# New instruction orders on four engines and a masked bias table in one GpSimd operation, in an attention and mixture-of-experts kernel

## What is computed

```python
xn = _layernorm(x)
# attention: scores times a 0/1 lower-triangular mask (masked scores are 0, not minus infinity)
q, k, v = xn @ Wq.T, xn @ Wk.T, xn @ Wv.T
attn = softmax((q @ k.T) * tril / sqrt(512)) @ v
# experts: the best 2 of 8 gates, renormalised
y[e] = xn @ We[e] + be[e]
ffn = sum over the two kept experts of gate[e] * y[e]
out = x + attn + ffn
```

## Time and profile before

| | before |
|---|---|
| median of 3 runs | 123.94 us (123.93 to 124.2) |
| the profiled execution's own time | 124.14 us |
| its span | 122.3 us |
| granted TensorE clock, mean | 0.998 |
| PE busy | 114.8 us, 94% of the span |
| weight loads (beside PE) | 103.6 us, 85% |
| VectorE (DVE) busy | 106.0 us, 87% |
| ScalarE (ACT) busy | 100.2 us, 82% |
| GpSimd (POOL) busy | 91.4 us, 75% |

### The profile page before, as it was taken

One profiled execution on the slowest core, in us unless ns is written; L12 is line 12 of the kernel. 1 busy time (PEld: TensorE's weight loads), 2 busy tenths in 40 slices (PEclk: granted clock), 3 DMA queues, 4 the chain that ended last, 5 costly groups with the idle time before them and its releaser, 6 DMA issues.

```text
span 122.3 us, 2940 instructions
## 1 busy us (share of the span) xinstructions
PE 114.8 (94%) x735; PEld 103.6 (85%) x735; DVE 106.0 (87%) x533; ACT 100.2 (82%) x338; POOL 91.4 (75%) x185
## 2 busy tenths in 40 slices
PE   4988959999999999999999999999999999989991
PEld 4857657998899998998899998999899989978890
DVE  0699858999989999898989998999989897869992
ACT  2465498989997999799987998799987999949950
POOL 7419848589947998499848996699849994677990
PEclk9999999999999999999999999999999999999999
DMA  3769400000200012000300020000300020000023
GB/s 98 245 195 300 106 3 5 0 3 3 86 0 0 3 29 62 0 0 3 91 3 0 0 82 9 0 0 5 88 0 0 5 86 0 0 3 0 21 73 86
DMA packets 9233, 5.18 MB, mean 42 GB/s; under 512 B 384, under 2 KB 9088, under 8 KB 9216
## 3 DMA queue, kind: packets, MB, share of 16 engines
q1 hardware_dynamic: 8656, 4.66, 13.4%
q10 hardware_dynamic: 560, 0.33, 1.0%
HBM read 2.89 MB, written 2.10 MB: 41 GB/s over the span
## 4 chain that ended last, share of the span: by engine, by line
PE 70%; POOL 11%; DVE 7%; ACT 5%; issue 3%; DMA 2%; POOLq 1%; DVEq 0%; ACTq 0%
PE attb L305 12%; PE ring L247 11%; PE ring L251 11%; PE ring L248 11%; PE score L292 5%; PE score L251 3%; PE score L248 3%; PE score L247 3%; PE ring L323 2%; DMA x_all<-in_x_dram 2%; POOL ysc L1097 2%; PE ring L333 2%; ACT ysc L905 2%; POOL rhs_rows L1136 2%; PE attb L357 1%
## 5 line engine op out<-in xcount | busy, mean ns | idle before, releaser
L905 ACT ACTIVATE ysc<-ring,gate 128x128 f32<-128x128 f32 x124 | 35.6, 385 | 1.8 <-PE ring L251 1.6
L247 PE MATMUL ring<-w_hi,xT_hi 128*128 128x512 f32 (+2 forms) x96 | 34.8, 363 | 0.0
L251 PE MATMUL ring<-w_hi,xT_lo 128*128 128x512 f32 (+2 forms) x96 | 32.7, 340 | 0.2 <-DVE xT_lo L508 0.2
L248 PE MATMUL ring<-w_lo,xT_hi 128*128 128x512 f32 (+2 forms) x96 | 32.5, 339 | 0.0
L1094 POOL TENSOR_TENSOR ysc<-ysc 128x256 f32<-128x256 f32 x31 | 22.8, 735 | 13.0 <-ACT ysc L905 13.0
L1097 POOL TENSOR_TENSOR ysc<-ysc,mix 128x256 f32<-128x256 f32 x31 | 22.8, 735 | 4.4 <-DVE mix L575 2.1
L575 DVE SCALAR_TENSOR_TENSOR mix<-ring,gate,mix 128x128 f32<-128x128 f32 x65 | 22.3, 345 | 0.4
L305 PE MATMUL attb<-c_s,probT 128*128 128x128 f32 x152 | 22.5, 278 | 0.0
L305 PEld LDWEIGHTS attb<-c_s,probT 128*128 128x128 f32 x152 | 20.4, 192 | 0.9
L247 PEld LDWEIGHTS ring<-w_hi,xT_hi 128*128 128x128 f32 x96 | 18.1, 189 | 2.4 <-DVE mix L575 0.5
L924 ACT ACTIVATE prob<-score,nmx 128x128 f32<-128x128 f32 (+3 forms) x32 | 17.7, 554 | 2.6 <-DVE nmx L624 1.8
(11 more groups left out here) (114 smaller groups left out, 242.3 us busy)
## 6 DMA issues: line engine op xcount, KB each, us to landing
x_all<-in_x_dram SPq DMA_DIRECT2D x7, 256.0 KB, 4.3
out_dram<-o_s SPq DMA_DIRECT2D x7, 256.0 KB, 2.3
w_f<-in_w_stacked_dram SPq DMA_DIRECT2D x1, 256.0 KB, 4.4
w_f<-in_w_stacked_dram SPq DMA_DIRECT2D x1, 192.0 KB, 4.2
w_f<-in_w_stacked_dram SPq DMA_DIRECT2D x1, 132.0 KB, 3.2
x_all<-in_x_dram ACTq DMA_DIRECT2D x1, 128.0 KB, 2.9
x_all<-in_x_dram SPq DMA_DIRECT2D x1, 128.0 KB, 2.7
wqk_s<-in_w_attention_dram ACTq DMA_DIRECT2D x1, 128.0 KB, 3.4
```

Of the source, the lines that this page charges most:

```text
L247: nc.tensor.matmul(dst, hi, w_h, start=True, stop=False)
L248: nc.tensor.matmul(dst, hi, w_l, start=False, stop=False)
L251: return nc.tensor.matmul(dst, lo, w_h, start=False, stop=True)
L905: last = nc.scalar.mul(ysc[:, t, e, :], bank(f"A{t}", b)[:, e * P:(e + 1) * P], gate[:, b % 2, t, e:e + 1])
```

## The change

The `WARM` counts go from 6 and 4 to 8 and 1. The bank order and the orders of PE, DVE, ACT and POOL are new in all three phases. At the start, B's low part moves from VectorE to GpSimd and A's high part moves ahead of batch 0's tokens on ScalarE. Batch 1's load waits for C's landing instead of B's, and the loads of batches 2 to 7 now wait for A's. `bias_rhs` becomes `bias_rhs_split` (a copy, a product and a sum over all 128 partitions) and `bias_rhs_blocks` (one product with four mask columns, behind the power for batch 1); the four 32-partition sums and the clearing of `rhs_rows` go. In the loop each engine's instructions per stage stay the same. The core of the diff, with the inner functions that only wrap the same code left out:

```diff
-WARM = (6, 4)
+WARM = (8, 1)
...
-FIRST_GROUPS = """C0@0 U@0 C1@0 C2@0 C3@0 SV@0 B0@0 A0@0 X@1 A1@0 B1@0 C0@1 C1@1 U@1 C2@1 A2@0""".split()
-GROUPS = "B2- C3 A3- B3- SV DT- A0 B0 X+ A1 B1 C0+ U+ C1+ C2+ A2".split()
-LAST_GROUPS = """B2@-2 C3@-1 A3@-2 B3@-2 DT@-2 SV@-1 A0@-1 B0@-1 A1@-1 B1@-1 B2@-1 A2@-1 B3@-1 A3@-1 DT@-1""".split()
+FIRST_GROUPS = """C0@0 C1@0 U@0 C2@0 C3@0 SV@0 B0@0 A0@0 X@1 A1@0 B1@0 U@1 C0@1 A2@0 C1@1 C2@1""".split()
+GROUPS = "B2- C3 A3- B3- SV DT- B0 A0 X+ A1 B1 U+ C0+ C1+ A2 C2+".split()
+LAST_GROUPS = """B2@-2 C3@-1 A3@-2 B3@-2 A0@-1 B0@-1 DT@-2 B1@-1 B2@-1 A1@-1 A2@-1 B3@-1 SV@-1 DT@-1 A3@-1""".split()
...
-        be_s = sb("be_s", [P, P + 1])
+        be_s = sb("be_s", [P, P + 1 + NT])
...
-            sp.wait_ge(S["w_b"], 16)
+            sp.wait_ge(S["w_c"], 16)
             sp.dma_start(x_all[:, NT * P:2 * NT * P].rearrange("p (t d) -> p t d", d=P), x_v[1]).then_inc(S["x1"], 16)
+            sp.wait_ge(S["w_a"], 16)
...
 
             wide(0, "C", 0)
+            wide(0, "C", 1)
             project_u(0)
-            wide(0, "C", 1)
             wide(0, "C", 2)
             wide(0, "C", 3)
+            value_sums(0)
             scores(0, 0)
             scores(0, 1)
-            value_sums(0)
             wide(0, "B", 0)
+            scores(0, 2)
             wide(0, "A", 0)
+            transpose_x(1)
             transpose_probs(0, 0)
-            scores(0, 2)
+            wide(0, "A", 1)
+            transpose_probs(0, 1)
             scores(0, 3)
-            transpose_x(1)
+            wide(0, "B", 1)
+            project_u(1)
+            wide(1, "C", 0)
+            wide(0, "A", 2)
             attend(0, 0)
-            wide(0, "A", 1)
-            wide(0, "B", 1)
-            wide(1, "C", 0)
-            transpose_probs(0, 1)
             wide(1, "C", 1)
-            project_u(1)
             wide(1, "C", 2)
 
             for n in range(1, B - 1):
                 wide(n - 1, "B", 2)
                 wide(n, "C", 3)
+                attend(n - 1, 1)
+                scores(n, 0)
+                transpose_probs(n - 1, 2)
                 wide(n - 1, "A", 3)
-                attend(n - 1, 1)
+                transpose_probs(n - 1, 3)
                 wide(n - 1, "B", 3)
-                transpose_probs(n - 1, 2)
-                scores(n, 0)
-                transpose_probs(n - 1, 3)
                 attend(n - 1, 2)
+                value_sums(n)
                 scores(n, 1)
-                value_sums(n)
                 transpose_rows(n - 1)
                 attend(n - 1, 3)
                 bias(n - 1)
+                wide(n, "B", 0)
                 wide(n, "A", 0)
-                wide(n, "B", 0)
                 scores(n, 2)
+                transpose_probs(n, 0)
                 transpose_x(n + 1)
-                transpose_probs(n, 0)
                 wide(n, "A", 1)
                 wide(n, "B", 1)
+                scores(n, 3)
+                project_u(n + 1)
...
-                wide(n + 1, "C", 0)
                 transpose_probs(n, 1)
-                project_u(n + 1)
                 wide(n + 1, "C", 1)
-                scores(n, 3)
                 wide(n + 1, "C", 2)
-                wide(n, "A", 2)
 
             wide(B - 2, "B", 2)
             wide(B - 1, "C", 3)
             scores(B - 1, 0)
             transpose_probs(B - 2, 2)
             wide(B - 2, "A", 3)
...
             scores(B - 1, 3)
             wide(B - 1, "B", 1)
+            attend(B - 2, 2)
             wide(B - 1, "B", 2)
-            transpose_probs(B - 1, 1)
+            attend(B - 2, 3)
+            wide(B - 1, "A", 1)
+            bias(B - 2)
             wide(B - 1, "A", 2)
             wide(B - 1, "B", 3)
+            transpose_probs(B - 1, 1)
+            value_sums(B - 1)
+            transpose_probs(B - 1, 2)
+            transpose_probs(B - 1, 3)
+            attend(B - 1, 0)
+            transpose_rows(B - 1)
             wide(B - 1, "A", 3)
-            transpose_probs(B - 1, 2)
-            attend(B - 1, 0)
-            transpose_probs(B - 1, 3)
             attend(B - 1, 1)
-            transpose_rows(B - 1)
             attend(B - 1, 2)
             bias_early(B - 1)
...
+            def first_sums(b):
+
+                dve.wait_ge(S["low_ready"], 1)
+                dve.wait_ge(S["xh_ready"], 1)
+                nc.vector.tensor_reduce(xs[:, 1:NT - 1], late_x[:, early].rearrange("p (t k) -> p t k", k=P), AX_X, ALU.add)
+                nc.vector.tensor_reduce(xs[:, 0:1], bank("X", 0)[:, P:2 * P], AX_X, ALU.add).then_inc(S["xsum_ready"], 1)
+
...
-            early, late = slice(0, 2 * P), slice(2 * P, NT * P)
-            dve.wait_ge(S["xh_early_ready"], 1)
-            split_lo(xT_lo[:, 0, early], bank("X", 0)[:, early], xT_hi[:, 0, early], S["xl_early_ready"])
-            dve.wait_ge(S["xh_ready"], 1)
...
+            first_sums(0)
+            x_lo_half(0, 1)
             normal_stats(1, 0)
             token_sums_pairs(0)
             normal_stats(1, 1)
             normal_stats(1, 2)
             normal_stats(1, 3)
+            normal_finish(1)
+            token_sums_later(0)
             u_lo(0)
-            token_sums_later(0)
-            normal_finish(1)
+            gate_max(0)
+            gate_drop(0)
             mask_scores(0, 0)
-            gate_max(0)
+            mask_scores(0, 1)
+            gate_below(0)
             negate_max(0, 0)
-            gate_drop(0)
-            gate_below(0)
+            negate_max(0, 1)
+            sv_rows(0, 0)
+            sv_rows(0, 1)
             gate_sum(0)
-            sv_rows(0, 0)
+            sv_rows(0, 2)
             gate_rec(0)
             gate_out(0)
-            sv_rows(0, 1)
-            sv_rows(0, 2)
             mix_b(0, 0, 0)
             mix_b(0, 0, 1)
-            mask_scores(0, 1)
             mix_b(0, 0, 2)
-            negate_max(0, 1)
             x_lo(1)
             token_sums(1)
...
                 mix_b(n - 1, 1, 0)
                 mask_scores(n - 1, 2)
                 mix_b(n - 1, 1, 1)
+                negate_max(n - 1, 2)
                 mix_b(n - 1, 1, 2)
-                negate_max(n - 1, 2)
-                token_sums_pairs(n)
+                u_lo(n)
                 normal_stats(n + 1, 0)
-                u_lo(n)
                 normal_stats(n + 1, 1)
+                normal_stats(n + 1, 2)
                 mask_scores(n - 1, 3)
-                token_sums_later(n)
                 mix_b(n - 1, 2, 0)
-                normal_stats(n + 1, 2)
                 mix_b(n - 1, 2, 1)
-                normal_stats(n + 1, 3)
                 negate_max(n - 1, 3)
                 mix_b(n - 1, 2, 2)
                 gate_max(n)
+                normal_stats(n + 1, 3)
                 gate_drop(n)
                 softmax_sum(n - 1)
+                token_sums_pairs(n)
                 softmax_tot(n - 1)
+                token_sums_later(n)
                 gate_below(n)
+                normal_finish(n + 1)
+                mix_b(n - 1, 3, 0)
                 mask_scores(n, 0)
-                softmax_rec(n - 1)
-                mix_b(n - 1, 3, 0)
-                normal_finish(n + 1)
+                mix_b(n - 1, 3, 1)
                 gate_sum(n)
                 negate_max(n, 0)
-                mix_b(n - 1, 3, 1)
+                mix_b(n - 1, 3, 2)
                 gate_rec(n)
+                softmax_rec(n - 1)
                 gate_out(n)
                 mask_scores(n, 1)
-                mix_b(n - 1, 3, 2)
-                negate_max(n, 1)
-                finish_tile(n - 1, 0)
                 sv_rows(n, 0)
                 sv_rows(n, 1)
+                mix_b(n, 0, 0)
                 sv_rows(n, 2)
+                mix_b(n, 0, 1)
+                finish_tile(n - 1, 0)
+                mix_b(n, 0, 2)
                 finish_tile(n - 1, 1)
-                mix_b(n, 0, 0)
+                negate_max(n, 1)
                 finish_tile(n - 1, 2)
-                mix_b(n, 0, 1)
                 finish_tile(n - 1, 3)
-                mix_b(n, 0, 2)
                 x_lo(n + 1)
                 token_sums(n + 1)
...
             softmax_sum(B - 1)
+            softmax_rec(B - 2)
             softmax_tot(B - 1)
+            mix_b(B - 1, 1, 2)
+            mix_b(B - 1, 2, 2)
+            finish_tile(B - 2, 0)
+            finish_tile(B - 2, 1)
+            finish_tile(B - 2, 2)
             mix_b(B - 1, 3, 0)
-            mix_b(B - 1, 2, 2)
+            finish_tile(B - 2, 3)
             mix_b(B - 1, 3, 1)
             mix_b(B - 1, 3, 2)
+            sv_rows(B - 1, 0)
+            sv_rows(B - 1, 1)
             softmax_rec(B - 1)
             mix_a(0)
+            sv_rows(B - 1, 2)
             mix_a(1)
             mix_a(2)
-            mix_a(3)
             finish_tile(B - 1, 0)
             finish_tile(B - 1, 1)
+            mix_a(3)
             finish_tile(B - 1, 2)
             finish_last(B - 1)
...
...
+            a_high(0)
+            wa_high(0)
+            x_hi_half(0, 0)
```

(80 more changed lines are left out.)

125 lines of the change are left out of this document (62 added, 63 removed).

## The result

The changed kernel takes 120.13 us (median of 4 runs, 120.04 to 120.22) against 123.94 us before (median of 4, 123.59 to 124.2): a ratio of 0.969, 95% interval 0.967 to 0.972, so 3.8 us or 3.1% faster. The forecast had the sign and the mechanism of the start right and was too small: 121.8 us, with 120.8 as the lower end of its range.

A forecast was written before the change was run, and what follows sets the result against it. The prediction took TensorE to bound the loop, with visible waits only in the start and end. Its terms, -1.4 (start), -0.3 (loop) and -0.4 (end), summed to -2.1 us: 121.8 us against 123.94, range 120.8 to 123.7.

The forecast's parts named there:

- Term 1: Start: earlier low part of A, power and batch 1 transposes, -1.4 us, ends 0.3 and 1.8 us of gain.
- (a): Start: GpSimd's subtraction for A's low part begins at 7.5 us instead of 8.88, 1.4 us earlier.
- (b): Start, GpSimd before the power: 2.4 us of bias table and B's low part replace 3.33 us, 0.9 less.
- (c): Start: power for batch 1 at 11.2 us instead of 13.51, so transposes possible at 14.4 instead of 16.70.
- (d): Start: TensorE is ready for batch 1's transposes at about 14.4 us; its earlier 0.61 us wait grows to about 1.2.
- Term 2: Six loop stages: the new order gains 0.05 us a stage, -0.3 us; lower end -1.0.
- Term 3: End: the 0.51 us wait for batch 6's bias rows goes, last A product later, -0.4 us; ends -0.9 and +0.5.
- slower rival: Loop: the third value row comes too late for the transposes in every stage, 125.7 us; chance 0.13.
- little start: Start: VectorE decides when batch 0's banks come free, nothing gained in loop and end, 123.4 us; chance 0.12.
- unchanged case: Start: normalisation stays where it was, loop at TensorE's pace as before, 123.9 us; chance 0.07.
- all of it at once: Whole kernel: 1.8 us from the start, 1.0 from the loop, 0.5 from the end, 120.7 us; chance 0.08.
- first products at half rate: Start: C triples and U at 1.2 GHz take 2.1 us more, about half hidden: 0 to +1.0, taken as 0.

The follow-up runs named there:

- e7: The kernel after with the old bias table in place of the new, ahead of B's low part and the power: 122.09 us.
- e2: The kernel before with the new loop orders of TensorE, VectorE and ScalarE and the loop's new bank order: 123.11 us against 124.04.
- e8: The kernel after with VectorE's pair sums and token sums moved back to about their old places in each stage: 120.30 us.
- e3: The kernel before with the change's end on all four engines: 123.25 us against 124.04.
- e11: The kernel before with the new loop orders of VectorE and ScalarE, TensorE's old: 132.96 us, ratio 1.070.
- e1: The kernel before with the change's start on all engines, including loads, dummy matmuls and bias table: 122.72 us against 124.04.
- e5: The kernel before with the value sums moved ahead of attend(n-1, 2) in TensorE's loop: 124.29 us against 123.95.
- e6: The kernel before with scores(n, 3) moved ahead of project_u(n+1) in TensorE's loop: 125.37 us, ratio 1.011.
- e4: The kernel before with TensorE's new loop order and its banks alone: 131.71 us, ratio 1.062.
- e9: The kernel after with ScalarE's loop order of the kernel before: 126.70 us, ratio to before 1.021.
- e10: The kernel after with VectorE's loop order of the kernel before: 122.86 us, ratio to before 0.989.
- e12: The kernel after with the sum of the bias split moved behind the power for batch 1: 120.42 us, ratio to before 0.970.

## Why the prediction was right or wrong

**What bounds the kernel**: right as far as it went. The loop goes at TensorE's pace in both kernels, and the start and the end had the visible waits. Wrong was the reading that the loop had no waits of TensorE, and that the room of the other engines was worth nothing there.

**Term 1, the start, -1.4**: right, measured -1.69 on the traces. (a) 7.60 us for a forecast of 7.5. (b) 1.3 us for the three operations up to 10.13 and 1.00 for B's part, for a forecast of 1.4 and 1.0. (c) the power at 11.20, as forecast; the variance was ready only then, held up behind B's part on GpSimd (0.75 us for an operation of 0.17, the row at 10.36), a wait that the prediction did not have. (d) the transposes at 14.33 for 14.4, with TensorE there at the same time; its wait ahead of the value sums was 0.94 us, for 1.2. The first B product came at 20.13 for 20.2 to 20.6: the 0.1 taken off for VectorE behind the transposes was not needed. Run e7 shows the term's main part directly, 1.96 us.

**Term 2, the loop, -0.3**: this is the step that failed; it measured -1.49. The prediction counted 13.1 us from the columns against 13.47, had the room of 0.35 us a stage (its own numbers give 0.37, 2.2 us over six), and then gave it away with the sentence "since the windows show no idle TensorE, I expect most of the 0.35 to be short matmuls that don't reach 0.454 ns a column, not waits". The chain shows the opposite: 0.23 of the 0.37 were waits, in three places, each 0.1 us or less in the stage shown, and run e2 has the shorter stage from the loop's orders alone. Short matmuls are only the remaining 0.14, of which the 128-column score triple has 0.11. The lower end, -1.0, was half of what the same paragraph allowed, and it is one reason why the range stopped short of the result. Term 2 is 1.2 of the 1.7 us by which the sum was short; the start is 0.3 and the end 0.2.

**The two-tensor operations counted at nothing in the loop**: right, by run e8 and by the stages of before, which are as long with the hold-up as without. In e8 the pair sums and the totals only changed places in waiting for GpSimd. Whether GpSimd waits in turn, which was the other half of the rule weighed there, was not measured.

**Term 3, the end, -0.4**: right in kind, -0.60 on the traces and -0.8 alone (e3). The 0.51 us wait before the transposed bias rows is gone. The late A product is not free: its sums on VectorE (L591) stand in the chain that ended last, from 113.45 us on. What it costs is inside the 0.60 and not separated.

**The slower rival** did not come about: the transposes have no wait in any stage of after. Its mechanism is real, as run e11 shows, where VectorE's new order meets TensorE's old one: there the transposes wait for the third value row in each stage. The little start and the unchanged case are out by the same rows as term 1. The case "all of it at once", 120.7 us, was nearest to the result and still too slow.

**The dummy matmuls** were counted at nothing, and no row speaks against it. They were changed in e1 together with the rest and not alone, so their price is not separated. But the case of first products at half rate can be read from the starts: in both kernels the first two matmuls of the first C triple start 0.23 us apart, those of U 0.23 and those of the next C triples 0.12. The last two are the distances of the loop, and the first is the same with either count of dummies. The granted clock reads 1.00 in each stretch of both starts. So the other count of dummies did not make these products slower.

**What stays open.** The stage of before is 13.47 us, although each of TensorE's waits in it can be moved. Runs e5 and e6 show that the next wait fills the room, and e4, e9, e10 and e11 that the new orders of TensorE, ScalarE and VectorE pay only together. The round through the bias matmul, VectorE and U's bank stands in every stage of before, but no run opens it alone. That the lead of the new start is kept only with the new loop (1.3 against 1.9 us at the first bias matmul) is measured and not taken apart. The gain of the end is measured as a whole (e3), and its parts are not separated.

## What to carry to other kernels

Compare the length of every piece of the bounding engine's chain with the price of its kind; a wait shorter than the overlap of two matmul records leaves the engine "busy" in every window, and three of them in a stage of 13.5 us were worth 1.4 us here. Then look for a round: an engine that waits for the bounding engine in each stage, and on which the bounding engine waits in turn. When a count from columns leaves a remainder, say which pieces it lies in before calling it a fixed cost, and keep the whole remainder in the range. Where several engines run hand-written orders, a short wait taken out in one of them tends to come back at the next semaphore, so change the orders together and judge them by the length of the stage.

## What the runs showed of the hardware that I had not expected

VectorE's addition of a constant to a 128x4 column (L504 after), with one SBUF input and not two, took 0.75 us instead of 0.17 while GpSimd subtracted on SBUF from 10.09 to 11.09. In runs e1 and e8 it took 0.45 and 0.44 beside the same subtraction, and in all three it ended 0.03 us behind it. In run e12, where the subtraction ended at 10.36, it took 0.17. So it is not only the operations on two SBUF tensors that are held up. The Trainium skill, SBUF — State Buffer, Who interferes with whom, says that a `tensor_scalar`, which this is, can run in a mode that takes both of VectorE's ports and then excludes GpSimd, the first to be issued holding them. The 0.75 us agrees, though no row shows the mode.

A GpSimd operation over 32 partitions is no cheaper than one over 128. The group of before that filled the bias table, by its line (ns min/median/max):

```profile
L1136 POOL TENSOR_TENSOR rhs_rows<-be_s,be_hi x4: 442/452/460, 11.2 to 12.8; 32x128 fp32r<-32x128 f32 x4
```

Its 452 ns stand beside 463 for the 128x128 sum, so four sums by 32 partitions cost 1.8 us, and the one sum and the masked product that took their place 0.46 + 1.05 = 1.5. The larger gain in the start is that the product (1.05 us) stands behind the power and not ahead of it.
